# Delta-rule chunk matrices packed 64 columns wide per head, with each batch on its own part of the TensorE array

## The chip, the cores and the metric

The kernel runs on one core of a Trainium2 chip. The metric is the device time of one execution in microseconds; lower is better. Everything is in float32.

## The reference

The model is a feed-forward half block, an attention block and the same feed-forward half block again, each added to the residual `x` of 2 batches, 512 tokens and 256 channels. The time is spent in the attention, which has 16 heads of 128 channels and a gated delta rule with a decay per channel:

```
q, k = silu(conv4(l2norm(h Wq))), silu(conv4(l2norm(h Wk)));  v = silu(conv4(h Wv))
beta = sigmoid(h Wb);   g = -exp(A_log) * softplus(h Wfa Wfb + dt_bias)      # per channel
for each token t:                                                           # per batch and head
    S  = S * exp(g_t)[:, None]
    e  = v_t - k_t S
    S  = S + beta_t * k_t[:, None] * e[None, :]
    o_t = (q_t * 128**-0.5) S
out = (rmsnorm(o) * rms_scale * sigmoid(h Wga Wgb)) Wo
```

## The kernel before

**Groups and chunks.** The 16 heads are done in 4 groups of 4 heads (`G = 4`, index `u`). In a group there is first a stage of 8 items (4 heads by 2 batches): projections, norms, the convolution and the decays of 512 tokens (`project` on TensorE, `item` on VectorE and ScalarE). Then the 512 tokens of each batch are scanned in 8 chunks of 64 tokens (`C = 64`). A chunk holds 2 batches by 64 tokens = 128 rows for each head, and so a row of tokens of all four heads is `UN = 512` columns wide, ordered head, batch, token.

**A chunk matrix.** Within a chunk the token by token recurrence is replaced by matrices over pairs of tokens: `nmat` (written key against key, strictly lower), `aq` (written key against query) and `tt`, the inverse of the first. Before the change each of them is 128 by 128 for a head: both batches stand in one matrix, of which only the two 64 by 64 blocks on the diagonal are used, since the batches don't meet. Four heads make 512 columns.

**Levels.** The decay between two tokens is a product over the tokens between them. It is built by doubling: six levels, h = 1, 2, 4 ... 32. At level l, `level_products` multiplies keys by keys and queries (both in `kq`), VectorE then multiplies half of the columns of `kq` and of `ks` by the decay totals and forms the next totals (`decays`: L981, L983, L984), and `keep_pairs` copies the pairs of this level out of PSUM under a mask (`copy_predicated`, L989 and L990). The next level's product needs the scaled `kq` and `ks`. A second chain inverts the matrix level by level: `inverse_y` on TensorE, a subtraction on VectorE (L1019), `inverse_t` on TensorE in two parts (L703 and L707), two copies on ScalarE (L479 and L481), and then `inverse_y` of the next level.

**Slots.** The work is software-pipelined. Slot n does the levels and the inverse of chunk n (`step`) and, woven between them, the scan of chunk n - 1 (`scan`): `r` = keys by state (L730), the right side, `u` = inverse by right side (L753), the output (L743 and L764), the new state (L714), and the normalised, gated output times `Wo` (L794, L821). Near its end it does the head of chunk n + 1 (`following`): the broadcast of beta (L659), the diagonal (L667), and level 0. Each engine has its own list of instructions, written out by hand in `slot`, and runs it strictly in that order; semaphores tie the lists together. A group has 8 full or nearly full slots and a last one that only scans.

**Who does what.** In a slot TensorE runs some 30 groups of matmuls; a float32 matmul shows as two instructions, so one for each of four heads is 8 instructions. VectorE does decays, masked copies, the inverse's subtraction, the state and the gate. ScalarE does silu and copies out of PSUM. GpSimd does four kinds of 512-column products: the first inverse (L336), the decayed state (L343), the normalised output (L351), and query times key for the diagonal (L358).

## Time and profile before

| | |
|---|---|
| median of 3 runs | 1710.4 us (1701.67 to 1733.17) |
| span of the profiled execution, first to last instruction | 1705.8 us |
| TensorE, matmul busy, weight load busy | 1461.6 us (86%), 1185.9 us (70%) |
| VectorE, ScalarE, GpSimd busy | 1112.7, 560.4, 392.1 us |
| one slot in steady state | 34.26 us |

The profiled execution's own device time is not listed beside its span; the median stands 4.6 us above the span. Busy matmul time overlaps itself and the weight loads, since matmuls are pipelined, so the start of one group to the start of the next says more than a duration.

### The profile page before, as it was taken

What the parts mean: (1) busy time and instruction counts of PE and PEld (TensorE: products, weight loads), DVE (VectorE), ACT (ScalarE), POOL (GpSimd) and SP (SyncE); (2) the same over time, 40 slices, a digit from 0 to 9 for tenths busy, and PEclk for the clock granted to TensorE, in tenths of its full rate; (3) what the DMA queues carried; (4) which work ended last, traced back from release to release, by engine and by line L of the source; (5) the groups of instructions that cost most, each with busy time, mean ns of one, the idle gap of its engine ahead of it and who ended that gap; (6) DMA issues with size and microseconds to landing.
All of it is one profiled execution on the core that took longest, in us unless ns stands there. A gap on an engine that the chain in (4) does not pass through costs nothing.

```text
span 1705.8 us, 25673 instructions
## 1 busy us (share of the span) xinstructions
PE 1461.6 (86%) x9434; PEld 1185.9 (70%) x9434; DVE 1112.7 (65%) x2013; ACT 560.4 (33%) x1082; POOL 392.1 (23%) x351
## 2 busy tenths in 40 slices
PE   5786899999878699999978699999978599999977
PEld 4432788888733588888833488888853378888866
DVE  4399576667469567667549756766729856666742
ACT  1286222222268322122148422212228522222221
POOL 5034022212124112112124211221214311211210
PEclk8798899899999799899989799989989789999986
DMA  4000100000000010000000010000000000000001
GB/s 107 1 0 1 50 1 1 0 0 0 1 14 1 3 48 1 0 0 0 1 14 1 0 50 1 0 0 0 0 15 0 1 1 1 1 0 0 0 1 25
DMA packets 12493, 14.59 MB, mean 9 GB/s; under 512 B 3124, under 2 KB 8310, under 8 KB 12406
## 3 DMA queue, kind: packets, MB, share of 16 engines
q1 hardware_dynamic: 12406, 13.48, 2.7%
q8 instruction: 49, 0.80, 0.2%
q14 instruction: 38, 0.31, 0.1%
HBM read 12.43 MB, written 1.05 MB: 8 GB/s over the span
## 4 chain that ended last, share of the span: by engine, by line
PE 52%; DVE 25%; issue 19%; ACT 2%; POOL 1%; SPq 1%; DVEq 1%; POOLq 0%; DMA 0%; ACTq 0%
PE bank L653 9%; PE bank L707 8%; PE bank L703 8%; PE bank L690 5%; DVE qkv L950 4%; DVE ks L983 4%; PE bank L821 4%; DVE kq L981 3%; DVE tot L984 2%; PE bank L667 2%; PE bank L723 2%; PE bank L659 2%; PE bank L714 2%; DVE nmat L989 2%; DVE aq L990 2%
## 5 line engine op out<-in xcount | busy, mean ns | idle before, releaser
L653 PE MATMUL bank<-kq,ks 128*128 128x128 f32 x1536 | 231.6, 296 | 53.1 <-DVE tot L984 47.2
L981 DVE TENSOR_TENSOR kq<-kq,tot 128x512 f32<-128x512 f32 x160 | 138.4, 865 | 194.5 <-PE bank L653 191.4
L653 PEld LDWEIGHTS bank<-kq,ks 128*128 128x128 f32 x1536 | 200.9, 202 | 69.2 <-DVE tot L984 59.9
L629 PE MATMUL bank<-hT,gw 128*128 128x512 f32 x384 | 185.7, 621 | 38.1 <-DVE region L957 19.1
L950 DVE SCALAR_TENSOR_TENSOR qkv<-region,gchan,qkv 128x512 f32<-128x512 f32 x192 | 201.1, 1099 | 0.0
L371 POOL TENSOR_TENSOR qkv<-qkv,kq 128x509 f32<-128x509 f32 (+2 forms) x96 | 133.2, 1388 | 282.9 <-ACT qkv L454 277.9
L690 PE MATMUL bank<-region,nmat 128*128 128x64 f32 x1280 | 173.4, 280 | 2.3
L707 PE MATMUL bank<-tt,fmat 128*128 128x64 f32 x1280 | 170.6, 277 | 5.5 <-DVE fmat L1019 5.5
L629 PEld LDWEIGHTS bank<-hT,gw 128*128 128x128 f32 x384 | 73.6, 198 | 142.7 <-issue 103.7
L690 PEld LDWEIGHTS bank<-region,nmat 128*128 128x128 f32 x1280 | 163.6, 199 | 12.4 <-DVE nmat L989 7.5
L707 PEld LDWEIGHTS bank<-tt,fmat 128*128 128x128 f32 x1280 | 160.6, 195 | 7.5 <-DVE fmat L1019 6.0
L703 PE MATMUL bank<-fmat,tt 128*128 128x64 f32 x1024 | 142.2, 282 | 21.5 <-DVE fmat L1019 18.6
L703 PEld LDWEIGHTS bank<-fmat,tt 128*128 128x128 f32 x1024 | 126.1, 193 | 47.0 <-DVE fmat L1019 40.0
L336 POOL TENSOR_TENSOR tt<-ident,nmat 128x512 f32<-128x512 f32 x32 | 41.1, 1285 | 478.1 <-DVE nmat L989 478.1
L479 ACT ACTIVATE region<-bank 128x256 f32<-128x256 f32 x128 | 49.5, 387 | 242.5 <-PE bank L703 242.5
L481 ACT ACTIVATE tt<-bank 128x256 f32<-128x256 f32 x160 | 61.8, 386 | 197.0 <-PE bank L707 197.0
L494 ACT ACTIVATE region<-bank 128x512 f32<-128x512 f32 x32 | 19.1, 597 | 288.1 <-PE bank L753 288.1
L990 DVE COPY_PREDICATED aq<-masks,bank 128x256 f32<-128x256 uint8 x192 | 104.2, 543 | 0.0
L989 DVE COPY_PREDICATED nmat<-masks,bank 128x256 f32<-128x256 uint8 x192 | 100.4, 523 | 0.0
L1019 DVE TENSOR_TENSOR fmat<-ident,bank 128x256 f32<-128x256 f32 x160 | 66.4, 415 | 40.9 <-PE bank L690 40.5
L983 DVE TENSOR_TENSOR ks<-ks,tot 128x256 f32<-128x256 f32 x160 | 90.2, 564 | 0.0
L346 POOL TENSOR_TENSOR ssq<-ssq,eps_sum 128x4 f32<-128x4 f32 x32 | 6.4, 200 | 360.8 <-DVE ssq L1046 360.8
(156 smaller groups left out, 2419.6 us busy)
## 6 DMA issues: line engine op xcount, KB each, us to landing
gw<-in_L_attn_Wq SPq DMA_DIRECT2D x4, 512.0 KB, 4.0
gw<-in_L_attn_Wk SPq DMA_DIRECT2D x4, 512.0 KB, 5.0
gw<-in_L_attn_Wv SPq DMA_DIRECT2D x4, 512.0 KB, 6.0
gwo<-in_L_attn_Wo SPq DMA_DIRECT2D x4, 512.0 KB, 4.9
x<-in_L_attn_hidden_states SPq DMA_DIRECT2D x2, 512.0 KB, 6.1
gfb<-in_L_attn_Wfb SPq DMA_DIRECT2D x4, 256.0 KB, 6.2
ggb<-in_L_attn_Wgb SPq DMA_DIRECT2D x4, 256.0 KB, 7.3
out<-x SPq DMA_DIRECT2D x2, 512.0 KB, 5.5
```

The source lines that it names most:

```text
L371: eng.tensor_tensor(o, o, vtap[tap][:, 0:S - shift], ALU.add).then_inc(v_chain, 1)
L629: last = eng.matmul(bank[t][:, :], gw[:, t, kt, cols], hT[:, kt, toks], start=(kt == 0), stop=(kt == KT - 1))
L653: last = eng.matmul(o[:, :, u, :].rearrange("p a (n t) -> p a n t", t=h), unit(ks[:, p], u), half(kq[:, p, :, u * P:(u + 1) * P], h, 1), s ...
L690: last = eng.matmul(bank[2][:, u * C:(u + 1) * C].rearrange("p (n t) -> p n t", t=h), unit(nmat[:, l], u), half(unit(tmat, u), h, 0), star ...
L703: last = eng.matmul(bank[3][:, u * C:(u + 1) * C].rearrange("p (n t) -> p n t", t=h), unit(tt[:, p], u), half(unit(fmat[:, l - 1], u), h, ...
L707: last = eng.matmul(bank[2][:, HU + u * C:HU + (u + 1) * C].rearrange("p (n t) -> p n t", t=h), unit(fmat[:, l - 1], u), half(unit(tt[:, p ...
L821: last = eng.matmul(bank[4][:, 0:HID], unit(oT, u), gwo[:, u, :], start=(u == 0), stop=(u == G - 1))
L950: last = eng.scalar_tensor_tensor(out=o, in0=src, scalar=w, in1=o, op0=ALU.mult, op1=ALU.add)
L981: eng.tensor_tensor(half(kq[:, p], h, 1), half(kq[:, p], h, 1), lower.rearrange("p (a n o) -> p a n o", a=1, o=1).broadcast_to((P, 2, nb, ...
L983: eng.tensor_tensor(half(ks[:, p], h, 0), half(ks[:, p], h, 0), spread(upper, h), ALU.mult)
L989: eng.copy_predicated(half(nmat[:, l], h, 1), mask, blocks(bank[l % 2][:, 0:HU], h)).then_inc(n_ready, 1)
L990: eng.copy_predicated(half(aq[:, p], h, 1), mask, blocks(bank[l % 2][:, HU:UN], h)).then_inc(aq_ready, 1)
```

## The change

**64 columns for a head.** All chunk matrices (`nmat`, `fmat`, `tt`, `aq`, `tmat`) become 64 columns wide for a head, 256 for four. Batch 0 has partitions 0 to 63 and batch 1 partitions 64 to 127. Each matmul over them becomes two, one for each batch: with 128 rows and 64 columns of the array for the level products and the diagonal, with 64 rows and 64 columns for the inverse, `u` and the output.

**Masked copies merged.** `nmat`, `aq` and `tt` are slices of one tensor `pairs`, and one `copy_predicated` of 2 by 128 columns takes the place of two of 256.

**Beta on the written key.** `ks` is now minus beta times key, and `kq` holds the bare key and query, made by one 1024-column product. The sign is turned back in the output weights.

**Value summed in PSUM.** The transposed value is put into bank 4 by a matmul with the identity, and `r` is added to it there. The subtraction L1031 and the scaling L1052 on VectorE are gone; ScalarE copies the result.

**Moves.** The decayed state, the normalised output and the first inverse leave GpSimd: ScalarE does the first two with 4 instructions for each 512 columns, TensorE and ScalarE the third. The new state of both batches is made by one batch-alternating group in two banks. The diagonal is the product of written key by query, 64 wide, and needs no GpSimd product.

The diff, cut:

```diff
-        nmat = sb("nmat", [P, NL, UN])
-        fmat = sb("fmat", [P, NL - 1, UN])
-        tt = sb("tt", [P, 2, UN])
-        aq = sb("aq", [P, 2, UN])
+        pairs = sb("pairs", [P, NL + 3, UC])
+        tt = pairs[:, TT0:TT0 + 2]
+        nmat = pairs[:, NMAT0:NMAT0 + NL]
+        aq = pairs[:, AQ0:AQ0 + 2]
+        fmat = sb("fmat", [P, NL - 1, UC])
...
+        def cell(ap, b, u):
+            return ap[b * C:(b + 1) * C, u * C:(u + 1) * C]
+        def tokens(b, u):
+            return slice(u * P + b * C, u * P + (b + 1) * C)
...
@@ gpsimd, slot
-                    eng.tensor_tensor(gd(tt[:, p]), ident4, gd(nmat[:, 0]), ALU.subtract).then_inc(tt0_ready, 1)
-                        eng.tensor_tensor(gd(sdec[:, b]), gd(state[:, b]), spread(decay, D), ALU.mult).then_inc(sdec_ready, 1)
-                    eng.tensor_tensor(gd(og), gd(og), spread(ssq[:, 2, :], D), ALU.mult).then_inc(on_ready, 1)
-                eng.tensor_tensor(kq[:, p, 1], ks[:, p], qs[:, :], ALU.mult).then_inc(qk_ready, 1)
@@ scalar, slot: new order
+                def decay_state(b):
+                    for u in range(G):
+                        last = eng.activation(unit(sdec[:, b], u), unit(state[:, b], u), ACT.Copy,
+                                              scale=gamma[:, q, u * B + b:u * B + b + 1])
+                    last.then_inc(sdec_ready, 1)
+                if scan:
+                    eng.wait_ge(state_ready, B * m + g + 1)
+                    eng.wait_ge(updated, NL * n)
+                    decay_state(0)
+                    eng.wait_ge(r_done, n)
+                    eng.activation(rs, bank[4][:, :], ACT.Copy).then_inc(rs_ready, 1)
+                if step:
+                    eng.wait_ge(t0_done, n + 1)
+                    eng.activation(tmat, bank[3][:, UC:2 * UC], ACT.Copy).then_inc(tm_ready, 2)
+                if scan:
+                    decay_state(1)
...
                 if scan:
+                    eng.wait_ge(rms_ready, n)
+                    eng.wait_ge(og_ready, n)
+                    for u in range(G):
+                        last = eng.activation(unit(og, u), unit(og, u), ACT.Copy, scale=ssq[:, 2, u:u + 1])
+                    last.then_inc(on_ready, 1)
+                gates(7)
+                if step:
+                    inverse(4)
+                if scan:
                     eng.wait_ge(ot_done, n)
                     eng.activation(oT, bank[7][:, :], ACT.Copy).then_inc(ot_ready, 1)
@@ tensor
-                    last = eng.matmul(o[:, :, u, :].rearrange("p a (n t) -> p a n t", t=h), unit(ks[:, p], u),
-                                      half(kq[:, p, :, u * P:(u + 1) * P], h, 1), start=True, stop=True)
+                    for b in range(B):
+                        last = eng.matmul(o[rows(b), :, u], ks[:, p, tokens(b, u)],
+                                          half(kq[:, p, :, tokens(b, u)], h, 1), start=True, stop=True)
...
+                def invert_pairs():
+                    for u in range(G):
+                        for b in range(B):
+                            last = eng.matmul(cell(bank[3][:, UC:2 * UC], b, u), cell(tt[:, p], b, u), id64[rows(b), 0:C],
+                                              start=True, stop=True)
+                    last.then_inc(t0_done, 1)
...
-                            last = eng.matmul(bank[3][:, u * C:(u + 1) * C].rearrange("p (n t) -> p n t", t=h),
-                                              unit(tt[:, p], u), half(unit(fmat[:, l - 1], u), h, 0), start=True, stop=True)
+                            for b in range(B):
+                                last = eng.matmul(o[rows(b), u], cell(tt[:, p], b, u), half(cell(fmat[:, l - 1], b, u), h, 0),
+                                                  start=True, stop=True)
...
+                    for u in range(G):
+                        for b in range(B):
+                            last = eng.matmul(unit(bank[4], u)[rows(b), :], kq[:, q, 0, tokens(b, u)], unit(state[:, b], u),
+                                              start=False, stop=True, skip_group_check=True)
...
-                    state_add(0)
-                if step:
+                            last = eng.matmul(unit(bank[6 + b], u), unit(kst, u)[rows(b), :], unit(us, u)[rows(b), :],
+                                              start=True, stop=True)
+                    last.then_inc(s_done, 1)
+                if step:
+                    eng.wait_ge(vs_ready, n + 1)
+                            last = eng.matmul(unit(bank[4], u)[rows(b), :], vs[:, tokens(b, u)], ident[:, :],
+                                              start=(u == 0), stop=False, skip_group_check=True)
+                    last.then_inc(vt_done, 1)
+                    level(4)
                     inverse_t(2)
-                    level(4)
@@ vector
-                eng.copy_predicated(half(nmat[:, l], h, 1), mask, blocks(bank[l % 2][:, 0:HU], h)).then_inc(n_ready, 1)
-                eng.copy_predicated(half(aq[:, p], h, 1), mask, blocks(bank[l % 2][:, HU:UN], h)).then_inc(aq_ready, 1)
+                eng.copy_predicated(half(o, h, 1), mask,
+                                    bank[l % 2][:, 0:UC].rearrange("p (a n t) -> p a n t", a=2, t=h)).then_inc(n_ready, 1)
...
-                eng.tensor_tensor(kq[:, p, 0], ks[:, p], bank[6][:, :], ALU.mult).then_inc(kb_ready, 1)
-                eng.tensor_tensor(kq[:, p, 1], qs[:, :], es, ALU.mult)
-                eng.tensor_tensor(kq[:, p, 0], kq[:, p, 0], es, ALU.mult).then_inc(kq_ready, 1)
-                eng.tensor_tensor(gd(aq[:, p]), ident4, spread(bank[5][:, 0:G], P), ALU.mult).then_inc(diag_ready, 1)
+                eng.tensor_tensor(kq[:, p], kraw[:, :, :], es.rearrange("p (o i) -> p o i", o=1).broadcast_to((P, 2, UN)),
+                                  ALU.mult).then_inc(kq_ready, 1)
+                eng.tensor_tensor(ks[:, p], kraw[:, 0], bank[6][:, :], ALU.mult).then_inc(kb_ready, 1)
+                eng.tensor_tensor(aq[:, p], id64[:, :], bank[1][:, UC:2 * UC], ALU.mult).then_inc(diag_ready, 1)
...
-                    eng.tensor_tensor(rs, vb, bank[4][:, :], ALU.subtract).then_inc(rs_ready, 1)
-                        eng.tensor_tensor(gd(tmat), ident4, gd(bank[2][:, :]), ALU.subtract).then_inc(f_ready, 1)
-                    eng.tensor_tensor(gd(vb), gd(bank[7][:, :]),
-                                      spread(btok[:, ds(c, 1), ds(g * G, G)].rearrange("p a h -> p (a h)"), D),
-                                      ALU.mult).then_inc(vb_ready, 1)
```

TensorE's order in a slot after the change is: `r`, level 1, `invert_pairs`, queries by state, level 2, `u`, y1, level 3, t1, output, y2, state, value, level 4, t2, y3, level 5, t3, transposed output, y4, beta, t4, transposed key, diagonal, y5, `Wo`, t5, level 0 of the next chunk.

## Rows read from the trace of the kernel before

**Rows 1.** The page, part 1: busy time, share, instructions of TensorE and VectorE.

```profile
PE 1461.6 (86%) x9434; PEld 1185.9 (70%) x9434; DVE 1112.7 (65%) x2013; ACT 560.4 (33%) x1082; POOL 392.1 (23%) x351
```

**Rows 2.** Windows, the stages of group 1: stretch, length, busy by engine, clock, DMA.

```profile
80.00:159.00 79.00, 69.46 (x152) 27.18 (x152) 71.21 (x91) 60.56 (x102) 30.45 (x23) 0.98 0.00 1
159.00:172.00 13.00, 2.04 (x9) 1.99 (x10) 9.10 (x12) 4.74 (x8) 4.11 (x3) 0.50 0.00 0
172.00:456.00 284.00, 264.04 (x2062) 244.07 (x2064) 182.10 (x368) 65.52 (x138) 55.19 (x52) 0.95 0.02 8
456.00:476.00 20.00, 9.85 (x56) 7.60 (x51) 3.92 (x10) 3.07 (x4) 2.25 (x3) 0.75 0.11 31
```

**Rows 3.** The page, part 4: the chain that ended last, by engine.

```profile
PE 52%; DVE 25%; issue 19%; ACT 2%; POOL 1%; SPq 1%; DVEq 1%; POOLq 0%; DMA 0%; ACTq 0%
```

**Rows 4.** Windows, one steady slot of group 2, gate product to gate product.

```profile
623.09:657.35 34.26, 31.80 (x266) 29.84 (x266) 23.87 (x48) 8.05 (x18) 7.44 (x7) 1.00 0.00 1
```

**Rows 5.** Timeline, TensorE groups of a steady slot: start, length, what.

```profile
640.54 1.34 PEld L730 LDWEIGHTS bank<-state,kq 128*64 128x64 f32 x16
...
650.28 0.97 PEld L703 LDWEIGHTS bank<-fmat,tt 128*128 128x128 f32 x8 [0.33 <-DVE fmat L1019]
...
651.17 0.97 PEld L707 LDWEIGHTS bank<-tt,fmat 128*128 128x128 f32 x8
...
652.06 0.97 PEld L653 LDWEIGHTS bank<-kq,ks 128*128 128x128 f32 x8
...
653.26 0.69 DVE L981 TENSOR_TENSOR kq<-kq,tot 128x512 f32<-128x512 f32 x1 [2.36 <-PE bank L653]
...
654.89 0.96 PEld L714 LDWEIGHTS bank<-region 64*128 64x128 f32 x8
...
655.97 0.97 PEld L703 LDWEIGHTS bank<-fmat,tt 128*128 128x128 f32 x8
```

**Rows 6.** Windows of one line's TensorE instructions: L604, then L730 twice.

```profile
71.60:74.90 3.30, 3.30 (x62) 3.30 (x63) 1.00 0.00 0
```

```profile
640.60:640.98 0.38, 0.38 (x4) 0.38 (x5) 1.00 0.00 0
641.08:641.46 0.38, 0.38 (x10) 0.38 (x8) 1.00 0.00 0
```

**Rows 7.** Timeline, VectorE and GpSimd in the same slots.

```profile
621.07 0.42 DVE L989 COPY_PREDICATED nmat<-masks,bank 128x256 f32<-128x256 uint8 x1
621.40 0.42 DVE L990 COPY_PREDICATED aq<-masks,bank 128x256 f32<-128x256 uint8 x1
621.89 0.69 DVE L1026 TENSOR_TENSOR state<-region,bank 128x512 f32<-128x512 f32 x1
622.49 0.68 DVE L1046 TENSOR_REDUCE ssq<-region 128x4 f32<-128x512 f32 x1
...
624.70 1.52 DVE L981 TENSOR_TENSOR kq<-kq,tot 128x512 f32<-128x512 f32 x1 [0.93 <-PE bank L653]
...
643.98 2.67 POOL L343 TENSOR_TENSOR region<-state,gamma 128x512 f32<-128x512 f32 x2
644.50 1.26 DVE L983 TENSOR_TENSOR ks<-ks,tot 128x256 f32<-128x256 f32 x1
645.68 1.12 DVE L984 TENSOR_TENSOR tot<-tot 128x128 f32<-128x128 f32 x1
```

**Rows 8.** Groups by line and form, ScalarE: count, busy, mean ns.

```profile
L479 ACT ACTIVATE region<-bank 128x256 f32<-128x256 f32 x128 | 49.5, 387 | 242.5 <-PE bank L703 242.5
...
L465 ACT ACTIVATE dec<-region,gnegA 128x512 f32<-128x512 f32 x32 | 22.8, 712 | 17.2 <-DVE region L967 17.2
...
L494 ACT ACTIVATE region<-bank 128x512 f32<-128x512 f32 x32 | 19.1, 597 | 288.1 <-PE bank L753 288.1
```

**Rows 9.** Windows, the scan of group 1, by granted clock.

```profile
213.50:302.20 88.70, 82.60 (x689) 77.45 (x688) 62.40 (x124) 21.03 (x44) 21.04 (x21) 1.00 0.00 1
302.20:305.60 3.40, 3.40 (x19) 3.40 (x18) 1.10 (x3) 0.98 (x2) 0.00 (x0) 0.50 0.00 0
```

More of the change, by code:

```diff
@@ L96, in build @@
         kst = part(6)
-        vb = part(7)
-        tmat = part(8)
+        vs = part(7)
+        tmat = part(8)[:, 0:UC]
         es = part(9)
@@ L735, in slot @@
                     level(1)
[L736 removed]
+                    invert_pairs()
                 gates(0, 1)
                 if scan:
[L739 to L745 removed]
+                    for u in range(G):
+                        for b in range(B):
+                            eng.matmul(unit(bank[5], u)[rows(b), :], kq[:, q, 1, tokens(b, u)], unit(state[:, b], u),
+                                       start=(u == 0), stop=False, skip_group_check=True)
@@ L746, in slot @@
                 if step:
                     level(2)
-                    inverse_y(1)
-                if scan:
-                    eng.wait_ge(rs_ready, n)
-                    eng.wait_ge(tt_ready, (NL - 1) * n)
-                    for u in range(G):
-                        last = eng.matmul(unit(bank[4], u), unit(tt[:, q], u), unit(rs, u), start=True, stop=True)
-                    last.then_inc(u_done, 1)
+                if scan:
+                    eng.wait_ge(const_ready, 1)
+                    eng.wait_ge(rs_ready, n)
+                    eng.wait_ge(tt_ready, NL * n)
+                    for u in range(G):
+                        for b in range(B):
+                            last = eng.matmul(unit(bank[4], u)[rows(b), :], cell(tt[:, q], b, u), unit(rs, u)[rows(b), :],
+                                              start=True, stop=True)
+                    last.then_inc(u_done, 1)
@@ L755, in slot @@
+                if step:
+                    inverse_y(1)
                 gates(2)
                 if step:
+                    level(3)
                     inverse_t(1)
-                    level(3)
                 gates(3)
                 if scan:
+                    eng.wait_ge(const_ready, 1)
                     eng.wait_ge(us_ready, n)
-                    eng.wait_ge(aq_ready, NL * n)
+                    eng.wait_ge(n_ready, NL * n)
                     for u in range(G):
-                        last = eng.matmul(unit(bank[5], u), unit(aq[:, q], u), unit(us, u), start=False, stop=True,
-                                          skip_group_check=True)
+                        for b in range(B):
+                            last = eng.matmul(unit(bank[5], u)[rows(b), :], cell(aq[:, q], b, u), unit(us, u)[rows(b), :],
+                                              start=False, stop=True, skip_group_check=True)
```

268 lines of the change are left out of this document (128 added, 140 removed).

## The prediction, made before the changed kernel was built

> **What bounds the kernel now.** I read the page's totals first: TensorE is busy 86% of the span with matmuls and 70% with weight loads, VectorE 65% [rows 1]. The windows of one group say where: of 396 us the scan of the 8 chunks takes 284 us, and there TensorE is busy 264 us, VectorE 182 us. The other stages are the items (79 us, untouched by the change), a passage of 13 us and a tail of 20 us [rows 2]. Four groups make 1136 us of scan, two thirds of the run. The chain that ended last runs over TensorE for 52% and VectorE for 25% [rows 3]. Then one steady slot: 34.26 us, weight loads 29.84 us of it, VectorE 23.87 us, ScalarE 8.05 us, GpSimd 7.44 us [rows 4]. So the slot is bound by TensorE's queue, with some 4.4 us of waits, and it is the weight loads that fill it: a group of 8 instructions whose loads are 128 columns starts its successor 0.89 us later (650.28, 651.17, 652.06), whether the moving side has 64 columns (L703, L707) or 128 (L653) [rows 5]. That is 0.111 us an instruction.
>
> **TensorE's queue, part by part.** First the prices. A load of 64 columns with 16 moving ones lets 63 instructions pass in 3.30 us, 0.052 us each [rows 6]. A 64-column load with 128 moving columns is the 16-instruction group L730: while only one batch's half of the array is in use, the window of 0.38 us shows a rate of about one each 0.11 us; in the middle, where the last of batch 0 and the first of batch 1 meet, twice as many records are in flight (10 against 4) [rows 6]. So two halves of the columns work at the same time. The change orders batches alternately, so I take two tiles as fully parallel: a group of 16 with 64-column loads and at most 64 moving columns costs 8 x 0.058 = 0.46 us (0.058 from the row's 0.052 with a little for the second stream), one with 128 moving columns 8 x 0.11 = 0.88 us. Bounds: 0.42 us, and 0.93 us if nothing overlaps, for the first; 0.88 and 1.76 us for the second. I take the low ones, because L730 is the nearest row.
>
> Per slot: six level groups fall from 0.89 to 0.46 (-2.6 us); fourteen inverse groups (5 y, 4 and 5 t) likewise (-6.0 us); L730 and L743 from 1.34 to 0.88 each (-0.9 us); the state from two groups of 0.89 to one (-0.9 us); the diagonal to 0.46 (-0.4 us). The value grows from a 4-instruction transpose, 0.44 us by half of 0.89, to 0.88 (+0.4 us); `invert_pairs` replaces a transpose of 0.44 by 0.46, `u` and output stay at 0.88 to 0.89. Sum -10.4 us. Against it stands the change of array shape: L714 uses 64 rows between groups of 128, and takes 1.08 us instead of 0.89, 0.19 for going in and out [rows 5], about 0.1 a change. Before there are some 10 changes in a slot, after, by the order of the groups, 19: +0.9 us. TensorE's queue needs 29.84 - 10.4 + 0.9 = 20.3 us.
>
> **VectorE.** Successive 512-column operations start 0.60 us apart (621.89, 622.49), the two masked copies of 256 columns 0.33 us apart [rows 7]. Merged copies take away 6 x 0.33 = 2.0 us; L1031, L1052 and the first inverse 3 x 0.6 = 1.8 us; the inverse's subtractions are halved (5 x 0.14 = 0.7 us); the diagonal's product is halved (0.3 us); the head's 1024-column product costs what its two predecessors did. Sum -4.8 us. GpSimd's 512-column work disturbs VectorE: L981 takes 1.52 us where a quiet one takes 0.69 [rows 5, 7]; L983 takes 1.26 and L984 1.12 beside L343 [rows 7], against about 0.42 and an estimated 0.28. That is 2.5 us, with the masked copies about 3 us a slot, and it goes with GpSimd's work. VectorE ends at about 16 us busy: no bound.
>
> **ScalarE** gets 12 instructions of 128 columns with a scale from memory. From 256 to 512 columns an activation grows from 387 to 597 ns, and a scale from memory adds about 100 ns (712 for L465) [rows 8]; so one of 128 is about 280 + 80 ns, 0.30 us start to start, four 1.2 us, twelve 3.6 us. With the copies of `rs`, `tmat` and `tt` and the shorter inverse copies it is busy some 11 us of a slot. Not a bound, but in order, so it can hold others.
>
> **What is late next.** With TensorE at 20.3 us the chain decides, and I walked one slot by these prices, with 0.25 us from a group's last matmul to its reader (652.06 to 653.26 is 1.20 us for an 0.89 us group [rows 5]). Zero is the start of the level 0 decays. A round of level product (0.7) and decays (0.6 + 0.33 + 0.2) is 2.0 us, so level 3's result is there at 6.2. Level 4 stands behind t1, output, y2, state and value in the queue, 4.0 us of work, and its result comes at 10.8 rather than 8.2; VectorE at that time does two state additions, the reduction and the gate, 2.4 us, so level 5's result comes at 13.8. Next ScalarE normalises the output in four pieces behind the third inverse's copies (15.0 to 16.2), and the transposed output stands ahead of y4 in TensorE's queue: y4 17.2, the beta group, t4 19.1. The copies of t4, then of the transposed output, hold the transposed key until 20.3; then diagonal, y5, `Wo` (1.7), t5, and level 0 with its result at 24.7. The shape changes lie on this path for some 14 groups: +1.4, 26.1. To that I add 2 us for the clock. In rows 9 the clock is at 2.4 GHz over 88.7 us and then at 1.2 GHz for 3.4 us, with TensorE shown busy the whole time around it [rows 9]. After the change the stretch from 14 to 21 us in my walk has small matmuls and waits, and I expect the lower clock in part of it; 3 to 4 us at that clock cost about 2 us by the rates of rows 9 (19 instructions in 3.40 us, 0.18 us each, against 0.11). Period: 28.2 us.
>
> **Sum.** The scan's 284 us are 8 periods of 35.5 us [rows 2], which hold the steady 34.26 and the slower first and middle ones. I set 28.3 against it: 7.2 x 8 x 4 = 230 us. In the passage TensorE waits for the GpSimd product of the diagonal, 1.3 us, which is gone, and the tail is shorter by about 1 us in `r`, output and state: 2.3 x 4 = 9 us. Preparation of masks is moved to narrower work in GpSimd's idle time, under the first feed-forward, at no cost; if it were late it would cost some us once. 1705.8 - 239 = 1467 of span, and 4.6 us more for the median: **1471 us**.
>
> **Rivals.** (a) *Halves of the rows don't work in parallel when they write the same PSUM bank.* `L730` shows two column halves, with all 128 rows; no row shows two row halves at once. The inverse, `invert_pairs`, `u` and the output use the two diagonal quarters and write one bank, the state writes two. If those groups run serially, 15 of them cost 0.93 instead of 0.46 (+7.0 us) and two 1.76 instead of 0.88 (+1.8 us): the queue needs 29 us, and with waits a period is about 32.5 us: 3.0 x 32 + 9 = 105 us less than before, 1605 us. Against it: the two quarters use different partitions of the bank. The Trainium skill states it as a rule (TensorEngine Tiling (Array Packing), Gotcha 1: PSUM Pressure): different row tiles cannot access the same bank at the same time. No run here shows that yet.
> (b) *The clock stays low in the scan.* Place: all slots, since quarter-array matmuls with 32 moving columns and gaps replace full ones. The evidence for it is that the clock already fell in a slot in which TensorE was fully busy [rows 9], against it that such falls are short and few (0.95 mean over the scan [rows 2]). Price: 20.3 us of queue becomes 32.5 us (x 1.6, rows 9) to 40.6 us (x 2); with waits up to 43. At 43 the kernel is slower by 7.5 x 32 = 240 us, 1940 us. It decides for slower from the point where the low clock covers about half of a slot (7.2 us gained, 14.8 us lost over a whole slot); with a quarter of the slot low the time is 1590 us.
> (c) *No tile overlaps at all, since float32 or the alternating order prevents it*: 23 groups stay at 0.93 and four at 1.76: the change's -10.4 us vanishes, VectorE's relief and the waits pay for the shape changes, and the time is 1690 to 1740 us, no change. L730's middle speaks against it.
> (d) *The chain is shorter than walked*, 24 us: ScalarE's normalising and the clock cost nothing. 11.5 x 32 + 9: 1333 us.
>
> **Chances.** Forecast (periods 26 to 30.5) 0.52; (a) 0.17; (b) partly 0.12, wholly 0.05; (c) 0.05; (d) 0.09. The range reaches from a period of 25 us (1705.8 - 345 + 4.6 = 1365) to a bit past (a) with the doubt in its waits: 1365 to 1640 us. Slower by over 2%, about what a measurement of this kernel can tell from no change, needs (b) wholly or a bad case of (c): 0.07; within 2% 0.06; faster 0.87.
>
> **What would show it.** Right: a slot of 26 to 30 us; inverse groups of 16 instructions starting 0.5 to 0.6 us apart when nothing waits; L730's successor 0.9 to 1.0 us after its first load; no VectorE instruction of 512 columns over 0.8 us; the wait ahead of the transposed output released by ScalarE. Wrong by (a): inverse groups near 0.93 us apart while level groups take 0.46; by (b): the clock of the scan windows at 0.8 or less; by (c): level groups at 0.93 us. The largest doubt is the walk: a hand-made order is only as good as its longest wait, and one instruction of ScalarE or VectorE that stands wrong costs a microsecond in each of 32 slots.

## The result and the profile after the change

| | before | after |
|---|---|---|
| median of 4 runs each, side by side | 1709.9 us (1701.7 to 1733.2) | 1611.6 us (1609.8 to 1614.0) |
| ratio, 95% interval | 1 | 0.944 (0.942 to 0.947) |
| span of the profiled execution | 1705.8 us | 1609.9 us |
| mean granted TensorE clock over the span | 0.919 | 0.818 |

Runs over 1.5% longer than the fastest of their kernel, which show a lower mean clock, are left out of the ratios.

The change is worth 98 us, less than half of the 239 us forecast. The time stands close to rival (a) (1605 us), but (a)'s mechanism isn't what happened, as the rows below show.

The page of the changed kernel: totals, the chain, and the instruction queue's line (packets, MB, share), which reads 49 packets and 0.80 MB on the page of before.

```profile
PE 1296.3 (81%) x16090; PEld 973.0 (60%) x16090; DVE 876.0 (54%) x1693; ACT 678.1 (42%) x1562; POOL 188.0 (12%) x204
...
q8 instruction: 153, 2.51, 0.7%
...
PE 58%; issue 18%; DVE 16%; ACT 6%; SPq 1%; DVEq 1%; POOLq 0%; DMA 0%; POOL 0%; ACTq 0%
```

Against [rows 1], TensorE has 70% more instructions and yet 165 us less matmul and 213 us less weight-load time; VectorE fell by 237 us. In the chain VectorE's share fell from 25% to 16% [rows 3], and ScalarE's rose to 6%. None of that tells why the time fell so little. The windows do: stretch, length, busy time of TensorE (matmuls, loads), VectorE, ScalarE, GpSimd, then the clock. First the four stages of group 1, then one steady slot, the stretch of low clock within it, the stretch of full clock behind that and the next stretch of low clock, a slot across the end of the loop body, and a gap in that slot.

```profile
80.00:158.00 78.00, 69.13 (x152) 26.86 (x152) 70.43 (x91) 60.08 (x101) 29.97 (x22) 0.98 0.00 1
158.00:171.00 13.00, 1.70 (x32) 1.73 (x32) 9.59 (x12) 5.24 (x8) 3.33 (x3) 0.51 0.00 0
171.00:440.00 269.00, 230.12 (x3746) 196.60 (x3742) 126.53 (x292) 94.86 (x255) 8.85 (x16) 0.78 0.03 10
440.00:458.00 18.00, 9.20 (x17) 5.08 (x18) 1.83 (x7) 3.68 (x7) 0.83 (x1) 0.64 0.11 33
383.59:414.08 30.49, 26.81 (x480) 23.57 (x477) 16.13 (x38) 11.50 (x31) 1.21 (x2) 0.83 0.01 2
390.40:400.60 10.20, 9.24 (x82) 7.79 (x81) 2.47 (x4) 1.64 (x4) 0.00 (x0) 0.50 0.01 2
400.60:417.70 17.10, 15.91 (x370) 14.33 (x368) 12.91 (x32) 6.86 (x20) 1.20 (x2) 1.00 0.02 3
417.70:431.40 13.70, 10.82 (x98) 8.64 (x100) 1.39 (x5) 3.00 (x9) 0.00 (x0) 0.50 0.00 0
242.79:281.75 38.96, 31.95 (x478) 28.13 (x474) 16.13 (x38) 11.84 (x32) 1.21 (x2) 0.69 0.01 3
264.35:267.50 3.15, 0.00 (x0) 0.00 (x0) 1.99 (x4) 0.88 (x4) 0.00 (x0) 1.00 0.02 5
```

Three things are to be seen. The scan stage fell from 284 us [rows 2] to 269 us, and its clock from 0.95 to 0.78. A steady slot takes 30.49 us instead of 34.26 [rows 4], and 10.2 us of it go by at 1.2 GHz. Of the sixteen full slots away from a jump, ten are like this one; the other six have 13.7 us at that clock (a mean of 0.79) and take 31.8 to 32.0 us, so that the same instructions take 1.5 us longer with 3.4 us more of it. And two of the seven slots of a group take 38 to 39 us: they contain some 3 us in which TensorE starts and executes nothing (3.15 us in the last row).

The timeline of the slot that begins at 402.26 us, which is the zero of the prediction's walk. It is the last full slot of the group, without a head for a next chunk, and its clock is low for 13.7 us from 417.7 on:

```profile
402.26 0.69 DVE L1031 TENSOR_TENSOR kq<-kq,region 128x512 f32<-128x512 f32 x1 [0.68 <-PE psum L696]
...
405.63 0.73 DVE L1043 COPY_PREDICATED pairs<-masks,psum 128x256 f32<-128x256 uint8 x1
...
407.34 0.60 PEld L739 LDWEIGHTS psum<-region,pairs 64*64 64x64 f32 x16
...
407.79 0.43 DVE L1043 COPY_PREDICATED pairs<-masks,psum 128x256 f32<-128x256 uint8 x1
407.98 0.55 PEld L696 LDWEIGHTS psum<-kq,ks 128*64 128x64 f32 x16
408.60 0.55 PEld L753 LDWEIGHTS psum<-fmat,pairs 64*64 64x64 f32 x16
...
409.06 0.56 PEld L759 LDWEIGHTS psum<-pairs,fmat 64*64 64x64 f32 x16
...
411.00 0.97 PEld L822 LDWEIGHTS psum<-region 64*128 64x128 f32 x16
...
412.09 0.85 PEld L829 LDWEIGHTS psum<-ident,region 128*64 128x64 f32 x16
...
416.64 0.69 DVE L1031 TENSOR_TENSOR kq<-kq,tot 128x512 f32<-128x512 f32 x1 [0.33 <-PE psum L696]
...
417.80 1.26 ACT L549 ACTIVATE region<-region,ssq 128x128 f32<-128x128 f32 x4
419.19 1.11 PE L844 MATMUL psum<-ident,region 128*128 128x128 f32 x4 [1.62 <-ACT region L549]
420.23 0.93 PEld L739 LDWEIGHTS psum<-region,pairs 64*64 64x64 f32 x16 [0.33 <-issue]
421.71 0.96 PEld L753 LDWEIGHTS psum<-fmat,pairs 64*64 64x64 f32 x16 [0.54 <-issue]
422.51 1.00 PEld L759 LDWEIGHTS psum<-pairs,fmat 64*64 64x64 f32 x16
424.57 0.72 PEld L861 LDWEIGHTS psum<-ident,ks 128*128 128x128 f32 x4 [1.05 <-issue]
```

The first half is what was forecast: L753 to L759 is 0.46 us for 16 instructions that load 64 rows by 64 columns, and both halves of the rows write the same PSUM bank, on different partitions. At 408.60 the array changes from 128 to 64 rows, and the step there is 0.62 us. From L844 on, the same two groups L753 and L759 need 0.96 and 1.00 us of load time instead of 0.55, at the clock of 0.50 of the window above. The gap at the end of the loop body, in the slot that takes 38.96 us:

```profile
263.22 0.93 PEld L696 LDWEIGHTS psum<-kq,ks 128*64 128x64 f32 x16
...
267.52 1.58 PEld L776 LDWEIGHTS psum<-state,kq 128*64 128x64 f32 x16 [3.37 <-issue]
```

L776 is `r`, the first group of the next pass of the loop over slots; no engine is named as what it waited for. The packets of the instruction queue say more than their total. From slot to slot of group 1, taken from VectorE's reduction to the next, there start 2, 1, 0, 0, 0, 1 and 2 of them before the change and 4, 6, 4, 6, 4, 4 and 2 after it, one at 264.80 us, for 0.93 of the 3.15 us of this gap. So before the change the loop's later passes fetched nothing, and now every pass fetches its instructions anew.

### The profile page after: what moved, and what is told of

It is laid out like the page before. It is cut to its first block, busy times and chain, and to the rows that moved or that the text cites. A ratio compares the mean times of both kernels' runs of the same rounds, so it can differ in the third digit from the quotient of the medians.

```text
span 1609.9 us, 38935 instructions
## 1 busy us (share of the span) xinstructions
PE 1296.3 (81%) x16090; PEld 973.0 (60%) x16090; DVE 876.0 (54%) x1693; ACT 678.1 (42%) x1562; POOL 188.0 (12%) x204
## 4 chain that ended last, share of the span: by engine, by line
PE 58%; issue 18%; DVE 16%; ACT 6%; SPq 1%; DVEq 1%; POOLq 0%; DMA 0%; POOL 0%; ACTq 0%
PE psum L696 7%; PE psum L870 7%; PE psum L739 5%; PE psum L759 5%; PE psum L753 4%; DVE qkv L999 4%; PE psum L702 3%; PE psum L786 2%; PE psum L768 2%; PE psum L822 2%; ACT region L549 2%; PE psum L796 2%; PE psum L861 2%; PE psum L712 2%; DVE state L1086 2%
## 5 line engine op out<-in xcount | busy, mean ns | idle before, releaser
L670 PE MATMUL psum<-hT,gw 128*128 128x512 f32 x384 | 186.6, 624 | 38.3 <-DVE gsel L1116 19.2
L696 PE MATMUL psum<-kq,ks 128*64 128x64 f32 x3072 | 143.2, 239 | 37.7 <-DVE tot L1034 31.6
L1031 DVE TENSOR_TENSOR kq<-kq,tot 128x512 f32<-128x512 f32 x160 | 110.5, 691 | 111.8 <-PE psum L696 110.0
L696 PEld LDWEIGHTS psum<-kq,ks 128*64 128x64 f32 x3072 | 123.3, 150 | 61.1 <-DVE tot L1034 43.3
L739 PEld LDWEIGHTS psum<-region,pairs 64*64 64x64 f32 x2560 | 108.8, 158 | 20.3 <-issue 14.2
L739 PE MATMUL psum<-region,pairs 64*64 64x32 f32 x2560 | 120.8, 239 | 0.1
L759 PE MATMUL psum<-pairs,fmat 64*64 64x32 f32 x2560 | 118.9, 237 | 1.7 <-issue 1.7
L870 PE MATMUL psum<-gwo,region 128*128 128x256 f32 x256 | 114.7, 626 | 2.7 <-ACT region L556 2.7
L759 PEld LDWEIGHTS psum<-pairs,fmat 64*64 64x64 f32 x2560 | 104.9, 156 | 16.0 <-issue 16.0
L1043 DVE COPY_PREDICATED pairs<-masks,psum 128x256 f32<-128x256 uint8 x192 | 102.0, 531 | 0.0
L753 PE MATMUL psum<-fmat,pairs 64*64 64x32 f32 x2048 | 95.3, 237 | 1.7 <-issue 1.7
L753 PEld LDWEIGHTS psum<-fmat,pairs 64*64 64x64 f32 x2048 | 80.8, 152 | 14.6 <-issue 7.6
L844 PE MATMUL psum<-ident,region 128*128 128x128 f32 x128 | 28.7, 364 | 65.7 <-ACT region L549 65.7
```

What stands on the lines that cost most here:

```text
L670: last = eng.matmul(bank[t][:, :], gw[:, t, kt, cols], hT[:, kt, toks], start=(kt == 0), stop=(kt == KT - 1))
L696: last = eng.matmul(o[rows(b), :, u], ks[:, p, tokens(b, u)], half(kq[:, p, :, tokens(b, u)], h, 1), start=True, stop=True)
L739: last = eng.matmul(o[rows(b), u], cell(nmat[:, l], b, u), half(cell(tmat, b, u), h, 0), start=True, stop=True)
L753: last = eng.matmul(o[rows(b), u], cell(tt[:, p], b, u), half(cell(fmat[:, l - 1], b, u), h, 0), start=True, stop=True)
L759: last = eng.matmul(o[rows(b), u], cell(fmat[:, l - 1], b, u), half(cell(tt[:, p], b, u), h, 1), start=True, stop=True)
L870: last = eng.matmul(bank[5][:, 0:HID], unit(oT, u), gwo[:, u, :], start=(u == 0), stop=(u == G - 1))
```

## The experiments

Theory A: the walk is right, and the missing time is clock. With the small matmuls TensorE does so little in the second half of a slot, above all while ScalarE normalises, that the clock falls. Theory B: TensorE's loop body got some 80% longer (480 matmul instructions in a slot for 266), and it has to be fetched again at each jump. Rivals: the fall comes with the one wait ahead of the transposed output and goes with it; the clock has no part, and fewer instructions or another order are what counts.

**e1, TensorE's slot loop written out.** The loops over groups and over pairs of slots become Python loops for TensorE, so that its list has no jump in the scan; each instruction stays the same.

```diff
-            with eng.Fori(0, NG) as g:
+            for g in range(NG):
...
-            with eng.Fori(0, NCH // 2 - 1) as w:
+                for w in range(NCH // 2 - 1):
```

> The changed kernel, with TensorE's list alone written out without loops (no jump; the other engines keep theirs). In the changed kernel a steady slot takes 30.4 us, and two slots of a group, the ones in which TensorE jumps back to the start of its loop, 38.8 us. Theory B, code: the loop's instructions no longer stay near the engine, and the jump costs 3.4 us without any instruction on TensorE, and then more at the lower clock. Then both long slots fall to 30.4 to 31 us, 8 x 8 us, and the time is about 1550 us. Rival, clock phase: the long slots come from where the lower clock falls, as the one of 40.4 us in the kernel before. Then they stay, and the time is 1600 to 1615 us. If straight code has to be fetched all the time and this is too slow, the time rises above 1620 us.

Measured: 1555.6 us, 0.911 (0.907 to 0.915) of before; 56 us less than the change. The slot of 38.96 us is the first of these, a steady one the second:

```profile
243.24:274.61 31.37, 27.63 (x476) 24.35 (x476) 16.30 (x37) 11.73 (x32) 1.21 (x2) 0.78 0.01 2
306.69:337.05 30.36, 26.74 (x478) 23.28 (x474) 16.13 (x38) 11.73 (x32) 1.21 (x2) 0.83 0.01 2
```

No slot is longer than 32.7 us, while the steady ones didn't move. That the jump costs this time is shown. It still fetches instructions in 128 packets, 3 or 4 in each full slot, so the fetching alone doesn't cost it. That TensorE waits for its instructions after a jump is the reading that fits the packets above; no row names it as the releaser.

**e2, extra full matmuls at the waits.** Eight matmuls of 128x128 by 256 columns a slot, in three places of TensorE's list: 3 ahead of the transposed output, 2 ahead of the transposed key, 3 ahead of the diagonal. Their results are not used.

```diff
+                def filler(k):
+                    eng.wait_ge(n_ready, NL * n + 5)
+                    for _ in range(k):
+                        eng.matmul(bank[0][:, 0:256], ident[:, :], gwo[:, 0, :], start=True, stop=True)
...
+                        filler(3)
...
+                        filler(2)
...
+                        filler(3)
```

> The changed kernel with added matmuls that compute nothing used (128 by 128 stationary, 256 columns, into a bank that is free there): three before the transposed output, two before the transposed key, three before the diagonal, where TensorE waits. Theory A, clock: the slot's second half is slow because the clock falls to 1.2 GHz for about 13.7 us of each slot after the waits; with the waits filled it stays at 2.4 GHz for most of the slot, and a steady slot falls from 30.4 us to 26 to 27.5 us, 1500 to 1540 us in all. Rival, chain: at that place other engines' round trips set the time and the clock costs little; the filler then only stands in the queue, and the slot takes 30.5 to 32 us, 1615 to 1660 us.

Measured: 1510.1 us, 0.884 (0.882 to 0.887); 101 us less than the change, with more work. The steady slot:

```profile
338.84:366.38 27.54, 26.24 (x494) 22.91 (x490) 16.10 (x38) 11.80 (x32) 1.21 (x2) 1.00 0.01 2
```

The clock is 1.00 through the slot, which is 2.95 us shorter; the two slots at the jump go from 38.8 to 34.2. Added work that does nothing but use the array saves 6% of the run. With e5 below, where the same places are filled and the slots follow the clock, this shows A as far as the cost of the clock goes. The rival that work on this path can only lengthen it has fallen.

**e3, y4 ahead of the transposed output.** TensorE does useful work where it waited for the normalising.

```diff
+                if step:
+                    inverse_y(4)
...
-                if step:
-                    inverse_y(4)
```

> The changed kernel with one group moved: the fourth inverse product ahead of the transposed output instead of behind it. Theory A: the 1.7 us wait for ScalarE's normalising no longer holds the inverse; the wait is shorter or gone, part of the low clock with it, and a steady slot falls by 1.5 to 3 us, 1525 to 1570 us. Rival: the transposed output is on the chain by itself (its copy holds the transposed key and the output product), so the slot gains at most 0.5 us, 1595 to 1611 us.

Measured: 1587.7 us, 0.931 (0.926 to 0.936); 24 us less than the change, and between the two expected ranges. The wait is still there, shorter:

```profile
387.19 1.11 PE L846 MATMUL psum<-ident,region 128*128 128x128 f32 x4 [1.01 <-ACT region L549]
```

The wait fell from 1.62 to 1.01 us, the steady slot from 30.49 to 29.84, and the clock of the span stays at 0.822. Both steady slots have the same mean clock of 0.83. So the gain is that of the order alone, and one wait shortened doesn't hold the clock.

**e4, batches one after the other.** The same instructions, in all twelve groups ordered batch, head instead of head, batch.

```diff
-                for u in range(G):
-                    for b in range(B):
+                for b in range(B):
+                    for u in range(G):
```

> The changed kernel with the order inside every group turned: all heads of batch 0, then all of batch 1, instead of the batches alternating. Same instructions, same tiles. If two tiles work at once only when neighbours in the queue use different ones, the groups of 16 go from 0.46 us towards 0.8 to 0.93 us at the high clock, 22 of them and four of 0.88 towards 1.3 to 1.76 us, 10 us more queue in a slot, less than that in the period since the fuller queue keeps the clock up: a slot of 33 to 38 us, 1690 to 1830 us. Rival: TensorE looks far enough ahead to overlap them anyway, as partly seen in the kernel before; then a slot stays within 1 us of 30.4 and the time within 1600 to 1640 us.

Measured: 1809.3 us, 1.059 (1.056 to 1.062): slower than before the change. A steady slot, and three groups of it:

```profile
385.13:422.48 37.35, 34.48 (x477) 31.16 (x475) 16.24 (x38) 11.78 (x32) 1.21 (x2) 0.82 0.01 2
```

```profile
424.41 0.80 PEld L739 LDWEIGHTS psum<-region,pairs 64*64 64x64 f32 x16
...
425.25 0.83 PEld L696 LDWEIGHTS psum<-kq,ks 128*64 128x64 f32 x16
...
426.15 0.62 PEld L753 LDWEIGHTS psum<-fmat,pairs 64*64 64x64 f32 x13
```

L739 and L696 now start their successors after 0.84 and 0.90 us; in the change the same two need 0.64 and 0.62 (407.34, 407.98, 408.60). This is rival (c)'s case, and worse than its 1690 to 1740 us, since the low clock (0.82 here too) and the jumps come on top: the change gains only because successive matmuls use different parts of the array.

**e5, the same extra matmuls on a quarter of the array.** As e2, with 64 rows and 64 columns. The two ahead of the transposed key stand before a wait for VectorE that they stood behind in e2.

```diff
+                        eng.matmul(bank[0][0:C, 0:256], ident[0:C, 0:C], gwo[0:C, 0, :], start=True, stop=True)
```

> The kernel with the filler matmuls, but each of them on one quarter of the array (64 rows, 64 columns) instead of all of it; same number, same 256 moving columns, same places. The full ones held the clock at 2.4 GHz and a steady slot at 27.55 us (1510 us). Theory A1, time: the clock is held by TensorE being occupied. Then the quarter ones do the same, a slot of 27.5 to 28 us, 1505 to 1525 us. Rival A2, share of the array: small matmuls count for little, the clock falls as in the changed kernel, and the filler is only more work at the lower clock: a slot of 31 to 33 us, 1620 to 1680 us.

Measured: 1608.4 us, 0.943 (0.938 to 0.948), as the change and in neither expected range. It is a mixture, two slots in a row:

```profile
355.51:383.26 27.75, 26.20 (x494) 21.89 (x490) 16.11 (x38) 11.78 (x32) 1.21 (x2) 1.00 0.01 2
383.26:417.13 33.87, 32.41 (x494) 25.74 (x490) 16.05 (x39) 11.55 (x31) 1.21 (x2) 0.80 0.01 2
```

Where the clock holds, a slot takes what e2's does; where it doesn't, the extra work costs 3.4 us above the change's 30.5. So it is the clock that e2 changed, not the order or the waits. Quarter-array matmuls of the same length and count hold it in 3 of the 16 full slots away from a jump, where e2's hold it in 14.

**e6, e1 and e2 together.**

> Both remedies in one kernel: TensorE's list without loops, and the filler matmuls. Alone they gave 1555.6 and 1510.1 us. If clock and code are two separate losses, the two long slots of a group (34.2 us with filler) fall to 27.6 us, 8 x 6.6 = 53 us: 1457 us. If they are one (the stall at the jump is what lowers the clock afterwards, and the filler has already paid for that), less than 20 us comes on top: above 1490 us.

Measured: 1449.3 us, 0.849 (0.847 to 0.850), 162 us less than the change; e1 and e2 alone sum to 157.5 us. All but one of the 24 full slots are now 27.4 us:

```profile
300.00:327.40 27.40, 26.23 (x494) 22.89 (x492) 16.06 (x38) 11.72 (x32) 1.21 (x2) 1.00 0.01 2
```

The two costs are separate and add up. The time is now within 1.5% of the forecast, but the forecast had already charged 64 us for the clock; what that leaves is counted below.

**e7, the order by hand, without extra work.** y4 first; the transposed key goes into bank 0 ahead of y4, so that it no longer follows the transposed output through bank 7; level 0 of the next chunk moves ahead of t5 and `Wo`, and its decays ahead of the residual's addition on VectorE; `r` behind level 1. ScalarE copies the transposed key right behind the normalising.

```diff
+                if step:
+                    eng.wait_ge(n_ready, NL * n + 5)
+                    for u in range(G):
+                        last = eng.transpose(unit(bank[0], u), unit(ks[:, p], u), ident[:, :])
+                    last.then_inc(kst_done, 1)
+                    inverse_y(4)
...
+                if following:
+                    eng.wait_ge(kst_ready, n + 1)
+                    level_products(n + 1, q, 0)
+                if step:
+                    inverse_t(5)
...
-                if step:
-                    inverse_t(5)
-                if following:
-                    level_products(n + 1, q, 0)
```

> The changed kernel in another order, with no filler and with the loops: the transposed key goes to bank 0 and no longer waits for the output's copy, the fourth inverse product goes ahead of the transposed output, level 0 of the next chunk goes ahead of the output product, the state product with the keys behind level 1, and the addition to x behind the next level 0. If waits and the clock that falls with them are the loss, TensorE's queue is filled by its own work: a steady slot of 24 to 26.5 us with the clock above 0.9, 1430 to 1510 us. Rival: the quarter-array work lowers the clock whatever the order; then the clock stays near 0.82 and a slot near 28 to 29 us, 1550 to 1580 us.

Measured: 1417.6 us, 0.830 (0.826 to 0.834), below the expected range and 194 us less than the change, though it still has the jumps. Of the 16 full slots away from a jump, 11 are like this one:

```profile
343.81:367.16 23.35, 22.45 (x478) 20.13 (x474) 16.12 (x39) 11.45 (x31) 1.21 (x2) 1.00 0.01 3
```

The loads fill 20.13 of 23.35 us, at full clock. The chain was in the order of the lists; with the waits gone most of the clock came back as well (a mean of 0.893 over the span for 0.818), unlike in e3, which removed only part of one wait.

**e8, the decayed state back on GpSimd.** ScalarE's 8 instructions become GpSimd's two 512-column products as before the change.

> The changed kernel with the decayed state back on GpSimd (two 512-column products a slot) instead of eight ScalarE instructions. In the kernel before, VectorE's decays beside it took up to 1.9 us longer a slot. If that disturbance was real and lies on the chain of the first half, a slot rises by 1 to 2 us and the time to 1640 to 1670 us. Rival: the second half of the slot sets the time and ScalarE is relieved of 2.5 us; then the time stays at 1600 to 1615 us.

Measured: 1611.4 us, 0.944 (0.941 to 0.947), no difference from the change. It doesn't test what it was made for. GpSimd takes up the state as soon as the decay totals are there, and then VectorE is idle for 2.5 us, so there is nothing to disturb:

```profile
387.35 2.04 POOL L369 TENSOR_TENSOR region<-state,gamma 128x512 f32<-128x512 f32 x2 [2.23 <-DVE gamma L1036]
```

What it does show is that ScalarE's 76 us of work (678 against 602 us busy) lay in nobody's way.

**e9, e7 and e1 together.**

> The reordered kernel (1417.6 us, steady slot 23.34 us) with TensorE's list without loops. Its slots at the jump take 28.4 to 30.5 us, now and then more. If code at the jump is a loss of its own, they fall to 23.3 to 24 us, 4 x (5 + 7) = 48 us: 1365 to 1380 us. Rival: with a queue this full, straight code can't be fetched fast enough (more than twice the instructions of the kernel before in two thirds of the time), stalls appear all along, and the time stays above 1400 us.

Measured: 1391.7 us, 0.812 (0.805 to 0.819), 12 us above the expected range and below the rival's; the jumps cost 26 us here. Two slots in a row:

```profile
286.54:309.77 23.23, 22.45 (x478) 20.13 (x474) 16.17 (x38) 11.72 (x32) 1.21 (x2) 1.00 0.01 3
309.77:337.54 27.77, 26.99 (x478) 23.79 (x474) 16.18 (x38) 11.66 (x32) 1.21 (x2) 0.82 0.01 2
```

Two or three of the six full slots of a group still lose the clock and 3 to 6 us with it. In the second, TensorE is shown busy for 26.99 of 27.77 us: the clock falls under a full queue of small matmuls too, with no wait that the good slot doesn't have. The two slots also price the clock: the same instructions take 4.5 us longer with 10.2 us of them at 1.2 GHz.

**e10, before the change with TensorE's slot loop written out.** The same edit as e1 on the kernel before.

> The kernel before the change with TensorE's list without loops. It has one slot of 40.4 us in each group, with the lower clock in it and no instruction fetches near it, and its jumps show no stall. If code was no loss there, the time stays within 5 us of 1710. Rival: the long slot comes from the jump after all; then it falls to 34.3 us and the time to 1686 us.

Measured: 1698.2 to 1754.2 us in 10 runs, with a median of 1726.2; the four within 1.5% of the fastest have a median of 1710.5, as expected, and the ratio is 1.0005 (0.994 to 1.007). In the traced run, of 1750.4 us, 8 of the 24 full slots take 40.4 to 43.7 us at a mean clock of 0.77 to 0.83, and in two groups none does. So which slots lose the clock varies here, and the ratio alone would hide a loss of up to some 10 us. The trace of before is plainer. The slot across its first jump, and one that loses the clock:

```profile
260.90:295.20 34.30, 31.83 (x267) 29.88 (x266) 23.89 (x49) 8.17 (x17) 7.43 (x7) 1.00 0.00 1
295.20:335.60 40.40, 38.08 (x267) 35.95 (x265) 23.84 (x49) 8.06 (x17) 7.42 (x7) 0.83 0.00 0
```

The first is as long as a steady slot and has no gap of 3 us, in any group. So the shorter body lost nothing that can be seen at the jump, and B is a cost that the change brought. The second is no matter of code: no instruction packet starts in it.

**e11, e9 with two full matmuls.** One matmul of 128x128 by 256 columns ahead of level 5, one ahead of the transposed key, results unused.

```diff
+                    eng.wait_ge(n_ready, NL * n + 4)
+                    eng.matmul(bank[1][:, 0:256], ident[:, :], gwo[:, 0, :], start=True, stop=True)
...
+                    for _ in range(1):
+                        eng.matmul(bank[0][:, 0:256], ident[:, :], gwo[:, 0, :], start=True, stop=True)
```

> The reordered kernel without loops (1391.7 us, slots of 23.2 us and, where the clock falls, 26.3 to 29 us, three of seven) with one full-array matmul of 256 columns ahead of level 5 and one ahead of the transposed key, results unused. In the stretch between them TensorE works without waits but on quarters of the array, and the clock falls in some slots. If light work is what lowers it, two full matmuls (0.9 us, 0.6 of it in waits) hold it up: all slots at 23.4 to 23.8 us, 28 slots x 0.9 us less, 1360 to 1378 us. Rival: the clock falls for a reason that this does not touch (its phase); then it falls as often, and the time is 1390 to 1405 us.

Measured: 1350.6 us, 0.789 (0.784 to 0.794), below the expected range, the fastest of all, 21% below before and 261 us below the change. All six full slots of a group, or five of them, look like this one:

```profile
283.56:306.92 23.36, 23.36 (x482) 20.80 (x478) 16.19 (x39) 11.76 (x32) 1.21 (x2) 1.00 0.01 3
```

A slot costs 0.13 us more than e9's good ones, and all but two of the 24 full slots are good. Whether it is the array that the two matmuls use or the waits that they fill was not tried apart here.

## Why the prediction was wrong, point by point

The time is in the range, and faster is right, but the size is off by 140 us. VectorE's reduction comes once a slot, and the distances between its starts split the 95.9 us by which the spans differ. Within a group there are seven:

- The six full ones sum to 211.7 us before, five of 34.26 and one of 40.4, and to 201.4 us on average after: 41 us gained in four groups, where 7.2 us each would be 173. Here 132 us are missing.
- The seventh belongs to a slot that makes no head for a next chunk. It was 23.34 us and is now 24.5 to 25.3: 7 us lost, where the sum took off 7.2 us in each of four groups, 29 us. Here 36 us are missing.
- What lies between the last one of a group and the first of the next went from 160.9 to about 145.9, 45.0 us in three; 15.6 us are gained ahead of the first and 1.6 behind the last. These 62 us are 24 more than the sum had for them.

So what is missing, and more, is missing in the slots. The steps of the prediction, one by one:

- *TensorE's queue, 20.3 us: right within 1 or 2 us.* The loads of a slot are busy for 20.13 us (e7, e9), and a group of 16 takes 0.46 us when nothing waits, so two tiles work in parallel. One price in it was too low: the change of array shape, taken as 0.1 us from L714's 0.19 [rows 5], costs 0.16 to 0.18 us (407.34 to 407.98 and 407.98 to 408.60, less 0.46), some 1.3 us more in 19 changes, of which part is gap and not in the 20.13.
- *VectorE, 16 us, ScalarE, 11 us: right*, at 16.13 and 11.50. No 512-column instruction is disturbed any more (0.69 us). But the masked copy of 0.73 us at levels 0 and 1 has nothing to do with GpSimd, which is idle then: it is 0.43 from level 2 on, so that the form of the copy sets it. That GpSimd's work was what disturbed VectorE before [rows 7] is supported by the row's going away with it, and no more; e8 didn't test it.
- *The walk: right to 1 or 2 us as far as the clock is full.* Level 5's result comes at 14.4 (13.8 forecast), the normalising runs from 15.5 to 16.8 (15.0 to 16.2), and the transposed output waits for ScalarE as forecast. Without its 2 us for the clock the walk gave 26.1 us; e6, at full clock, takes 27.4, with eight matmuls more.
- *"3 to 4 us at that clock cost about 2 us": this step failed.* 10.2 us of each steady slot are at 1.2 GHz, and 13.7 us in others. With the clock held, e2's slot is 27.54 us against 30.49, so it costs 2.9 us even with the added matmuls in it. In all the forecast charged 2 us in each of 32 periods, 64 us, and e2 gives back 101 us. The length came from [rows 9], where it was misread. The fall of 3.4 us shown there is the first of three in one slot, 13.6 us together, and the slot that holds them is the one of 40.4 us shown under e10, 6.1 us longer than its neighbours:

```profile
309.10:315.90 6.80, 6.80 (x28) 6.26 (x26) 2.23 (x4) 0.98 (x2) 0.00 (x0) 0.50 0.00 0
326.10:329.50 3.40, 3.40 (x18) 3.40 (x18) 2.23 (x7) 0.45 (x1) 0.00 (x0) 0.50 0.00 0
```

- *A term that was put at nothing: code.* The prediction counted instructions (16 for 8) only by TensorE's time for them, not by what a loop body of that size costs. At the end of a pass of the loop TensorE stands still for about 3 us and starts again at the lower clock (L776's loads take 1.58 us there and 0.86 us elsewhere); the two slots take 38.8 us instead of 30.5. e1 puts it at 56 us, and before the change nothing of it is to be seen. The page of before held one hint, 49 packets on the instruction queue for 32 slots: the loop fetched next to nothing while its body was short. Its one slot of 40.4 us in seven was a hint of the clock.
- *"7.2 x 8 x 4": the wrong base.* The 7.2 us are 35.5 - 28.3, and 35.5 is the mean of a stage that holds the slot of 40.4 us and other parts. A steady slot of 34.26 us had 6.0 us to lose by the prediction's own period, and the short seventh distance was given the same 7.2. It rose instead; with the clock held it is 20.5 us (e2) and in e7's order 18.2.
- *The account.* e6 has next to nothing of either cost and takes 1449 us, 162 us less than the change. Without its 64 us for the clock the forecast was 1407 us, 42 us below e6. So the 140 us are 162 - 64 + 42: code 56 us, clock about 40 us more than charged, and 42 us of periods that were too short for a slot at full clock. Up to 1.3 us a full slot, 32 us, of these 42 may be the walk's or the added matmuls' own cost; that wasn't separated.
- *Rival (b) named the mechanism*, and its sign, a clock of 0.8 or less in the scan windows, came true: 0.78. It priced "a quarter of the slot low" at 1590 us. A third of a steady slot and, by that mean, 44% of the scan stage turned out low; the 14.8 us that it took for a whole slot would be 5.0 us for that third, where e2 gives back 2.9. Presumably it cost less because part of the low time is waiting anyway.
- *Rival (a) is false*, though its 1605 us is nearest. The Trainium skill's rule (TensorEngine Tiling (Array Packing), Gotcha 1: PSUM Pressure) is that different row tiles cannot access one PSUM bank at the same time. Here L753's and L759's two batches lie on different row tiles and write one bank, at 0.46 us for 16, while (a) asked for 0.93. The measurement decides: for quarters on the diagonal of the array, which write different partitions of the bank, no such cost shows.
- *Rival (c) is false as the change is written*, and true under the other order (e4). *Rival (d), 1333 us*: the order of before cannot reach it, but e11 comes to 1351 with another order, without jumps and with the clock held: the chain behind level 5 was a matter of order and not of work.

Still open: why the clock holds in some slots of e5 and e9 and falls in others with the same instructions; whether TensorE's stand at the jump is the wait for instruction packets; what the 24 us outside the slots came from; how the 6.7 us by which e2's jump slots (34.2 us) exceed its steady ones divide, beyond the 3 us of standing still; and whether GpSimd's products would still disturb VectorE if both ran at once.

## What to carry to other kernels

When matmuls are made smaller and more numerous, price three things beside their own time: the granted clock in the stretches where they leave most of the array idle, the size of the loop body in instructions, and the waits that become the chain. Take what a step saves off the slots that contain it, one by one, and not off the mean of a stage. When a fall of the clock is found, look on to its end. Order tiles so that successive matmuls use different parts of the array: the same instructions in the other order cost 12% here (1611.6 against 1809.3 us). And when a result agrees with a rival's number, look for the rival's own mark (here 0.93 us for a group) before believing it.

## What the runs showed of the hardware that was not expected

- A TensorE with nearly no idle time can lose its clock: 26.99 of 27.77 us shown busy and a mean of 0.82 (e9), with quarter-array and half-array matmuls. Two full-array matmuls of 256 columns more in a slot held it (1.00) in 22 of the 24 full slots, and cost 0.13 us (e11).
- Matmuls whose results nobody needs made the kernel 6% faster (e2).
- With a loop body about 80% longer (480 matmul instructions in a slot for 266), the jump back costs 2.7 to 3.6 us in which TensorE does nothing (3.15 us in the window at 264.35). Written out without jumps, 128 packets of instructions come in without such a gap.
